# Sliding-window attention of a language-model layer: q and k parts stored once, a residual kept in on-chip memory, and mask tiles added by one wide matmul

## The reference

```
h = h + attn(layernorm(h))     # per head: keys within 64 positions, and apart from it the first 64 keys
h = h + ffn(layernorm(h))      # 8 experts, the best 2 of each token, 1280-odd slots per expert and 4096 tokens
```

```
local_mask = |idx_q - idx_k| <= 64
scores = where(local_mask, q @ k.T / sqrt(16), -inf)
out = (1 - gate) * softmax(scores) @ v + gate * softmax(q @ k[:64].T / sqrt(16)) @ v[:64]
return out @ Wout + bout
```

## Time and profile before

| | |
|---|---|
| time, median of 3 runs | 3890.7 us (3886.15 to 3896.99) |
| time of the profiled execution | 3882.3 us |
| its span, first to last instruction | 3880.6 us |
| mean granted TensorE clock | 0.952 |
| PE busy | 3481.5 us, 90% |
| DVE busy | 2172.5 us, 56% |
| POOL busy | 2324.1 us, 60% |
| ACT busy | 1868.3 us, 48% |
| HBM read, written | 198.55 MB, 192.88 MB |

### The profile page before, as it was taken

How to read it: one execution, slowest core, us unless ns; L and a number is a source line. 1 busy time by engine, 2 the same in 40 slices (tenths; PEclk the granted TensorE clock), 3 DMA queues, 4 the chain that set the end, 5 groups by cost and what they waited for, 6 DMA issues and landing times. The chain is left out here.

```text
span 3880.6 us, 117579 instructions
## 1 busy us (share of the span) xinstructions
PE 3481.5 (90%) x47537; PEld 2753.0 (71%) x47537; DVE 2172.5 (56%) x5392; ACT 1868.3 (48%) x3086; POOL 2324.1 (60%) x2599
## 2 busy tenths in 40 slices
PE   2898889888888888888899849999999999999998
PEld 1555555555555555555555539999999999999998
DVE  3576767767676776767677634343434344443333
ACT  0455555555555555555555624343444444444343
POOL 5566777777777777777776645444544444444443
PEclk7899999999999999999999969999999999999999
DMA  4354544445454444545454323232323233222222
GB/s 142 123 157 117 163 122 151 130 138 139 128 152 123 150 133 135 144 125 149 124 154 130 109 87 65 50 68 46 71 48 72 48 69 72 46 51 45 45 45 41
DMA packets 242540, 398.31 MB, mean 103 GB/s; under 512 B 34572, under 2 KB 150748, under 8 KB 242044
## 3 DMA queue, kind: packets, MB, share of 16 engines
q1 hardware_dynamic: 168540, 297.43, 25.0%
q0 software_dynamic: 70512, 91.16, 13.8%
q10 hardware_dynamic: 3008, 2.95, 0.2%
HBM read 198.55 MB, written 192.88 MB: 101 GB/s over the span
## 5 line engine op out<-in xcount | busy, mean ns | idle before, releaser
L1388 POOL DMA_INDIRECT out_y<-out_t,tok_out x264 | 425.7, 1612 | 747.3 <-DMA out_y<-out_t,tok_out 405.0
L1534 ACT ACTIVATE act<-psS 128x512 f32<-128x512 f32 x528 | 316.9, 600 | 882.1 <-PE psS L1462 880.9
L1596 DVE TENSOR_TENSOR h_lo<-act,h_hi 128x512 fp32r<-128x512 f32 x528 | 367.2, 695 | 562.3 <-ACT h_hi L1535 543.8
L993 DVE TENSOR_REDUCE negm<-psS 128x4 f32<-128x640 f32 x512 | 418.8, 818 | 452.3 <-remote 276.3
L903 ACT ACTIVATE pl<-psS 128x896 f32<-128x896 f32 x512 | 467.7, 913 | 379.9 <-PE psS L741 372.0
L568 POOL TENSOR_SCALAR_AFFINE_SELECT pl<-pl 128x512 f32<-128x512 f32 x512 | 354.3, 692 | 448.4 <-ACT pl L903 446.2
L1497 PE MATMUL psO<-w_hi,h_hi 128*128 128x256 f32 x2112 | 598.8, 284 | 0.8 <-DVE h_lo L1596 0.8
L1497 PE MATMUL psO<-w_lo,h_hi 128*128 128x256 f32 x2112 | 588.7, 279 | 0.0
L1497 PE MATMUL psO<-w_hi,h_lo 128*128 128x256 f32 x2112 | 587.6, 278 | 0.0
L1462 PE MATMUL psS<-xg_hi,w_hi 128*128 128x256 f32 x1984 | 551.7, 278 | 0.0
L1462 PE MATMUL psS<-xg_hi,w_lo 128*128 128x256 f32 x1984 | 551.5, 278 | 0.0
(11 more groups left out here) (232 smaller groups left out, 7728.6 us busy)
## 6 DMA issues: line engine op xcount, KB each, us to landing
qk_scr<-qk SPq DMA_DIRECT2D x64, 768.0 KB
Q<-qk_scr SPq DMA_DIRECT2D x128, 384.0 KB
K<-qk_scr SPq DMA_DIRECT2D x128, 384.0 KB
qk_scr<-qk SPq DMA_DIRECT2D x64, 512.0 KB
qk_scr<-qk SPq DMA_DIRECT2D x64, 256.0 KB
h_rows<-held SPq DMA_DIRECT2D x32, 512.0 KB
hb<-h_rows SPq DMA_DIRECT2D x32, 512.0 KB
x_rows<-x SPq DMA_DIRECT2D x32, 512.0 KB
```

What stands on the lines that cost most here:

```text
L993: dve.tensor_reduce(negm[:, g, 0, v, :, 2 * half:2 * half + 2], psS[:, 2:4, 0:2 * BAND].rearrange("p a (q u) -> p a q u", u=BAND), AX.X, A ...
L1388: pool.indirect_dma_start(out=y[:, :], in_=out_t[:, tile.out, s, :], in_offset=None, out_offset=bass.IndirectOffsetOnAxis(ap=tok_out[:, ti ...
L1534: act.activation(act32[:, b, :, 0:cols], src, ACT.Silu)
L1596: dve.tensor_tensor(h_lo[:, 2 * b:2 * b + 2, 0:cols], act32[:, b, :, 0:cols], h_hi[:, 2 * b:2 * b + 2, 0:cols].bitcast(F32), ALU.subtract) ...
```

## The change

Three things change, all in the attention stage. (1) `qk_scr` holds each part once; `qk_write` writes 128 rows of 2 KB six times for each sequence, and `load` builds the 96 rows of a quarter with three DMAs for `Q` (blocks 0 to 2 from part 1, 3 and 4 from part 2, 5 from part 3) and three for `K` (parts 1 to 3, parts 1 and 2, part 1). (2) `held` becomes a ring of four sequences, from which the projection's addition reads; the DRAM tensor, `hb` and SP's stages `hold` and `hb` go. (3) The four mask matmuls for each of the two heads of a max tile, with 32 identity columns each, become one with the whole identity.

```diff
-            for c in range(4):
-                last = pe.matmul(out[SUB * c:SUB * (c + 1), :, 0:5:4, :], identb[:, SUB * c:SUB * (c + 1)],
-                                 tri[:, :, 0:5:4, :], start=False, stop=True, skip_group_check=True)
+            last = pe.matmul(out[:, :, 0:5:4, :], identb[:, :], tri[:, :, 0:5:4, :],
+                             start=False, stop=True, skip_group_check=True)
...
-AT = {"q": ((0, 1, 3), (3, 2, 2), (4, 1, 1)), "k": ((2, 1, 3), (1, 4, 2), (0, 1, 1))}
+RUNS = ((0, 0, 3), (3, 1, 2), (5, 2, 1))
...
-    qk_scr = nc.dram_tensor("qk_scr", [2, ROWS, H, T], BF16, kind="Internal").ap()
+    qk_scr = nc.dram_tensor("qk_scr", [2, 3, HD, H, T], BF16, kind="Internal").ap()
...
-                first, step, n = AT["qk"[part]][term]
-                into = qk_scr[part].rearrange("(j d) (v a) t -> (d v) j (a t)", d=HD, a=2)
-                sp.dma_start(into[:, first:first + step * (n - 1) + 1:step, :],
-                             rows[:, 2 * part:2 * part + 2, :].rearrange("p a t -> p (a t)").unsqueeze(1).to_broadcast([P, n, 2 * T])
-                             ).then_inc(qk_out, 16)
+                sp.dma_start(qk_scr[part, term].rearrange("d (v a) t -> (d v) (a t)", a=2),
+                             rows[:, 2 * part:2 * part + 2, :].rearrange("p a t -> p (a t)")).then_inc(qk_out, 16)
...
-                for part, into in enumerate((Q, K)):
-                    sp.dma_start(into[0:ROWS, 4 * g:4 * (g + 1), :], qk_scr[part, :, 4 * g:4 * (g + 1), :]).then_inc(quarter_in[g], 16)
+                heads = slice(4 * g, 4 * (g + 1))
+                for first, term, n in RUNS:
+                    sp.dma_start(Q[first * HD:(first + n) * HD, heads, :],
+                                 qk_scr[0, term, :, heads, :].unsqueeze(0).to_broadcast([n, HD, 4, T])).then_inc(quarter_in[g], 16)
+                    sp.dma_start(K[first * HD:(first + n) * HD, heads, :],
+                                 qk_scr[1, 0:n, :, heads, :]).then_inc(quarter_in[g], 16)
...
-                need(pool, hold_out, 16 * s)
-            pool.tensor_tensor(held[:, arg, :], h[:, arg, :], bout_b[:, :], ALU.add).then_inc(held_done, 1)
+                need(pool, h1_done, 2 * (s - LIVE + 1))
+            pool.tensor_tensor(held[:, s % LIVE, arg, :], h[:, arg, :], bout_b[:, :], ALU.add).then_inc(held_done, 1)
```

More of the change, by code:

```diff
@@ L53 @@
 JOBS = 5 * QUARTERS
+LIVE = 4
 GROUPS = 3 * QUARTERS
@@ L103, in build @@
     lora_rows = nc.dram_tensor("lora_rows", [VG * GT, R], F32, kind="Internal").ap()
-    qk_scr = nc.dram_tensor("qk_scr", [2, ROWS, H, T], BF16, kind="Internal").ap()
+    qk_scr = nc.dram_tensor("qk_scr", [2, 3, HD, H, T], BF16, kind="Internal").ap()
     m_scr = nc.dram_tensor("m_scr", [QUARTERS, MAXROWS, 4, T], BF16, kind="Internal").ap()
-    h_rows = nc.dram_tensor("h_rows", [N, D], F32, kind="Internal").ap()
     x2_rows = nc.dram_tensor("x2_rows", [N + P, D], F32, kind="Internal").ap()
@@ L366, in build @@
             h = tmp("h", [P, QB, D])
-            held = tmp("held", [P, QB, D])
-            hb = tmp("hb", [P, QB, D])
+            held = tmp("held", [P, LIVE, QB, D])
             stats1 = tmp("stats1", [P, QB, 6])
@@ L430, in build @@
             la_t_ready, la_t_done, lora_ready = sem("la_t_ready"), sem("la_t_done"), sem("lora_ready")
-            h_done, held_done, hold_out, hb_in = sem("h_done"), sem("held_done"), sem("hold_out"), sem("hb_in")
+            h_done, held_done = sem("h_done"), sem("held_done")
             mv1_done, var1_done, xn_done = sem("mv1_done"), sem("var1_done"), sem("xn_done")
@@ L460, in build @@
             gates_done, xn_wg_done = sem("gates_done"), sem("xn_wg_done")
-            LOADS = 2 * 16
+            LOADS = 2 * len(RUNS) * 16
             GATHERS = 2 * QB * 16
@@ L533, in build @@
             ORDER["sp"] = (
[L534 to L538, removed]
+                ("prev", "m_out", 3), ("cur", "load", 1), ("prev", "m_in", 3), ("cur", "load", 2), ("past", "x2", None),
+                ("cur", "m_out", 0), ("cur", "m_in", 0), ("cur", "load", 3), ("cur", "m_out", 1), ("nxt", "qk_write", (0, 0)),
+                ("nxt", "qk_write", (0, 1)), ("nxt", "qk_write", (0, 2)), ("cur", "m_in", 1), ("nxt", "qk_write", (1, 0)),
+                ("nxt", "qk_write", (1, 1)), ("nxt", "qk_write", (1, 2)), ("nxt", "load", 0), ("cur", "m_out", 2),
+                ("past", "y", None), ("cur", "m_in", 2),
             )
@@ L627, in _ @@
                     x2_seq = x2_rows[0:N, :].rearrange("(s q p) d -> s p q d", q=QB, p=P)
-                    h_seq = h_rows.rearrange("(s q p) d -> s p q d", q=QB, p=P)
                     for stage, arg, s in order("sp"):
@@ L1141, in _ @@
                             if arg == 0:
-                                dve.wait_ge(hb_in, 16 * (s + 1))
+                                dve.wait_ge(held_done, QB * (s + 1))
                                 need(dve, y_out, 16 * s)
@@ L1145, in _ @@
                                               psX[:, b, :].rearrange("p (q d) -> p q d", q=2),
-                                              hb[:, 2 * arg:2 * arg + 2, :], ALU.add).then_inc(h1_done, 1)
+                                              held[:, s % LIVE, 2 * arg:2 * arg + 2, :], ALU.add).then_inc(h1_done, 1)
                         if stage == "stats2" and arg == 0:
```

## The result

The changed kernel takes 3966.9 us (median of 4 runs, 3965.7 to 3976.3) against 3890.2 us of the kernel before (3886.2 to 3897.0): a ratio of 1.0201, 95% interval 1.0179 to 1.0222. That is 77 us slower. I had said 3916 and a range up to 3958; the sign was right, but by luck: the size and the reason were not.

A forecast was written before the change was run, and what follows sets the result against it. PE was taken to set the attention stage's pace, with short spells at DVE's. Masks +29 us and shorter waits for load 0 -3 made +26, loads and h plus bias nothing: 3916 us, range 3870 to 3958.

The forecast's parts named there:

- I cost the loads at nothing, and what hides them is that room: Loads of Q and K: 8.8 to 12.3 us each, hidden by the time before PE's first use; cost nothing.
- rival (b): Broadcast loads come late, engines 0 and 1 set max tile 0: +60 us at the upper end, 3947 middle; chance 0.20.
- The masks, +0.9 us an iteration (+29 us): Local max tiles: width changes at five tiles and later maxima cost 0.5 to 1.35 us an iteration, taken as 0.9.
- The overlap: Behind the new mask line, before an exp or out group: an overlap of 0.07 and not 0.21 us.
- Rival (a): Masks cost nothing lasting, width changes falling in PE's idle time: 0.3 us or less an iteration, 3880 to 3901; chance 0.20.
- Rival (c): Faster: PE's issue idle before the masks, 1.6 us an iteration, goes; net -0.7 us, 3868; chance 0.18.
- The writes: Writes of q and k: load 0 goes 1.5 to 2.4 us earlier, taken as 2.0; its short waits go, -3 us.
- h plus bias: DRAM write and read of 512 KB each a sequence: removing them worth nothing but for freer DMA engines.
- The sum: Whole kernel: masks +29 us, short waits for load 0 -3, together +26; 3908 against the profiled execution, said as 3916.
- PE waiting for Q or K at L691, DMA share low while a load runs, with few engines at work: Next profile, attention stage: the sign that would show the forecast for the loads wrong.
- an iteration of 68.3 us: Next profile, attention stage: a sign of the forecast being right, with 67.4 us an iteration before.
- The mask line: Next profile: a sign of being right, L706 with 1024 matmuls where L715 had 4096.

The follow-up runs named there:

- a3: The kernel before with only the q and k part changed: parts written once, loads by six DMAs, Q by broadcast reads; ratio 1.0258.
- a4: The changed kernel with Q read by one DMA for each block of 16 rows; ratio to the kernel before 0.9953.
- a1: The kernel before with only the masks changed, one whole-identity mask matmul for each head; ratio 0.9954.
- c2: The kernel before with the whole identity only at the eleven local max tiles followed by 128-column work; ratio 0.9931.
- a2: The kernel before with only the ring of held in SBUF, no DRAM write and read of h plus bias; ratio 0.9997.
- e1: The kernel before, each quarter loaded by six DMAs of 48, 32 and 16 rows, none by broadcast; ratio 1.0064.

## Why the prediction was wrong

- **"I cost the loads at nothing, and what hides them is that room": this step failed.** The arithmetic of the load held: I had 8.8 to 12.3 us on two or three engines and it took 10.0 in the load shown and 10.4 to 11.4 by the medians. The room was a little less than I had, 9.5 us in the load shown in place of 10.3 to 10.5, in part because I took the first use for the time at which PE was ready, 0.44 us of waiting included. PE's own wait for K is 6.5 us in 11.4 sequences, 0.6 an iteration, below the 1 us of rival (b). What I left out is that a load slow on two or three engines can be in the way of others. I asked of each load only whether its own reader has room, and wrote that loads 1 to 3 have more. With four loads of 10 us in 70 one is in flight more than half the time, and gathers, scatters, maxima and the writes of `x_rows` go meanwhile and were late: DVE's wait for the scatters went from 0.3 to 11.3 us, a write of `x_rows` from 5.9 to 8.0. a3 and a4 size the term: +100 us, where I had 0 and rival (b) 60 at the most. Rival (b) was right that the loads decide; the wait that it named is 0.6 us of the 2.4 an iteration in the changed kernel. How the rest divides among the late transfers is open.
- **The masks, +0.9 us an iteration (+29 us): wrong sign.** a1 measured -18 us. The overlap was read rightly: behind the wide masks, ahead of an exp or out group, it is 0.07 us (median of the 33 places in the 800 us), where I had said 0.07 and not 0.21. That it costs time isn't shown (c2 against a1 has the sign, within intervals that overlap), and if it does it is made up for: PE waited less for DVE, 18.1 us before L699 in a1 against 27.1. Rival (a) had named this. Rival (c) had the sign and -0.7 us an iteration (a1: -0.56), yet not the mechanism: the "issue" idle before the masks went to other lines.
- **The writes: right.** SP's wait for them fell from 25.9 us to 5.2 in 6 times, the longest 1.2, and the earlier start brought no time: a4 equals a1.
- **h plus bias: right.** a2 0.9997.
- **The sum** of +26 us was thus two errors of opposite sign, 0 for +100 and +29 for -18, and its own sign came out right by luck: the term that gave it had the wrong one. With both terms as measured the sum is 3890 + 100 - 18 = 3972, near the 3967 of the changed kernel.
- **The signs I had named**: "PE waiting for Q or K at L691, DMA share low while a load runs, with few engines at work" came true, and an iteration of 68.3 us did not. The mask line has its fourth of the matmuls (x364 in 11.4 sequences, 32 each), and the granted clock of the 800 us did change: 0.93 in place of 0.95.

## What to carry to other kernels

Look at the slowest count of a DMA's pattern. In this kernel a leading broadcast of 3 and 2 copies left the end of a load to about two engines, and 6 blocks with gaps left a load to 5.9 of 16; either cost 2.6%, though DMA engines were idle half the time before. When a transfer becomes slow, ask not only whether its reader has room but what else is in flight beside it: quarter 3, with the most room, did more harm than quarter 0, with the least. And idle time named "issue" before a line isn't that line's: test whether it goes or moves before counting on it.

## What the runs showed of the hardware that I had not expected

- The kernel before took 3879 to 3892 us in five sessions and 3687 and 3676 us in two, one of these on a chip that in another session gave 3881. In the short sessions the thin spell is gone: in e1's trace the eight transposes of `xn` run in one piece right behind tile 11, without an "issue" gap.

```profile
1154.06 0.45 PE L701 MATMUL psS<-K,Q 96*32 96x160 bf16 x16
...
1154.56 1.09 PE L854 MATMUL psX<-ident,xn 128*128 128x128 f32 x8
```

  POOL's row of indirect DMAs is the same there, so it isn't that row alone that starves PE. What does is open.
- DVE's waits with no releaser in the records, 112 us in 800 of before, are absent in e1's trace as well.
- With PE waiting more in each iteration the granted clock of the same 800 us was lower, 0.93 after and 0.95 before, so a wait may have cost more than its length. How much more wasn't measured.
